# A tail in which half of each batch's base products stand behind the next batch's scan transposes, and ScalarE makes means and variances from row sums

## What is computed

```
x = x + tanh(g_xattn[0]) * L0_xattn(ctx, layernorm(x))      # scan, gated by silu(layernorm(x))
x = x + tanh(g_ffn[0])   * L0_moe(layernorm(x))             # 16 experts, top 4
x = x + tanh(g_xattn[1]) * L1_xattn(ctx, layernorm(x))
x = x + tanh(g_ffn[1])   * L1_ffn(layernorm(x))
# L1_ffn(x):  x @ base_w.T + base_b + 2 * ((x @ lora_A) * gate) @ lora_B,
#             gate = top 2 of softmax(x @ router_w.T + router_b), 8 experts of rank 16
# layernorm(x) = (x - mean) / sqrt(var + 1e-5), over the 512 channels of a token
```

## Time and profile before

| | |
|---|---|
| median of 3 runs | 1531.58 us (1530.7 to 1533.62) |
| profiled execution, its own time | 1533.84 us |
| its span, first to last instruction | 1532.0 us |
| mean granted clock of TensorE | 0.942 |

### The profile page before, as it was taken

One profiled execution on the slowest core, in us unless ns is written; L12 is line 12 of the kernel. 1 busy time (PEld: TensorE's weight loads), 2 busy tenths in 40 slices (PEclk: granted clock), 3 DMA queues, 4 the chain that ended last, 5 costly groups with the idle time before them and its releaser, 6 DMA issues.

```text
span 1532.0 us, 14502 instructions
## 1 busy us (share of the span) xinstructions
PE 1278.9 (83%) x4518; PEld 726.6 (47%) x4518; DVE 1408.5 (92%) x1468; ACT 838.0 (55%) x1344; POOL 788.3 (51%) x411
## 2 busy tenths in 40 slices
PE   7785796899699867986889999899988888836998
PEld 3331232443244323442457666566665666625555
DVE  4999999999999999998899999999899999987894
ACT  5754657574755465634865665546556444424442
POOL 0465456445644553460475456655566666555642
PEclk9898899899989998998899999999999999967999
DMA  8364456535544553460367678677786888754531
GB/s 254 107 142 126 112 131 144 136 110 140 138 139 93 143 133 100 97 171 23 90 178 235 233 244 281 228 273 234 240 262 227 276 260 289 249 191 143 169 105 56
DMA packets 99836, 264.30 MB, mean 173 GB/s; under 512 B 10832, under 2 KB 11344, under 8 KB 93616
## 3 DMA queue, kind: packets, MB, share of 16 engines
q1 hardware_dynamic: 87936, 225.36, 50.6%
q0 software_dynamic: 11440, 37.50, 7.3%
q10 hardware_dynamic: 384, 0.52, 0.1%
HBM read 233.73 MB, written 29.62 MB: 172 GB/s over the span
## 4 chain that ended last, share of the span: by engine, by line
DVE 43%; PE 22%; issue 10%; DMA 6%; POOL 5%; ACT 2%; DVEq 0%; SPq 0%; ACTq 0%; POOLq 0%
DVE state L1667 18%; DVE banks L1659 12%; PE banks L1137 7%; DMA expert_w<-in_moe_w 3%; PE banks L1148 3%; DMA ys_d<-expert_out 2%; PE banks L1047 2%; DVE y_scan L1678 2%; POOL state L451 2%; PE banks L1096 1%; PE banks L1104 1%; DVE du L1379 1%; DVE hidden L1685 1%; PE banks L1305 1%; PE banks L1116 1%
## 5 line engine op out<-in xcount | busy, mean ns | idle before, releaser
L451 POOL TENSOR_TENSOR state<-state,bc_rows 128x1024 f32<-128x1024 f32 x254 | 598.7, 2357 | 639.7 <-DVE banks L1659 639.5
L1047 PE MATMUL banks<-state,ident 128*128 128x512 f32 x640 | 332.9, 652 | 109.7 <-POOL state L451 109.6
L1667 DVE TENSOR_TENSOR_SCAN state<-decay,banks 128x1024 f32<-128x1024 f32 x176 | 402.1, 2285 | 7.5 <-ACT decay L681 3.0
L1659 DVE TENSOR_TENSOR banks<-du,bc_rows 128x1024 f32<-128x1024 f32 x256 | 314.7, 1229 | 12.8 <-issue 0.5
L1137 PE MATMUL banks<-z_gate,expert_w 128*128 128x256 f32 (+1 forms) x1504 | 284.6, 347 | 7.7 <-DMA expert_w<-in_moe_w 7.7
L1137 PEld LDWEIGHTS banks<-z_gate,expert_w 128*128 128x128 f32 x1504 | 249.7, 191 | 61.7 <-issue 20.6
L681 ACT ACTIVATE decay<-delta,neg_a 128x511 f32<-128x511 f32 x352 | 230.7, 712 | 49.2 <-DVE state L1667 45.9
L1047 PEld LDWEIGHTS banks<-state,ident 128*128 128x128 f32 x640 | 119.6, 200 | 290.4 <-POOL state L451 176.7
L1667 DVE TENSOR_TENSOR_SCAN state<-expert_w,banks 128x1024 f32<-128x1024 f32 x80 | 182.9, 2286 | 3.8 <-ACT expert_w L681 1.1
L1148 PE MATMUL banks<-expert_w,hidden 128*128 128x512 f32 x316 | 158.3, 616 | 2.9 <-DVE hidden L1688 2.9
L1678 DVE TENSOR_TENSOR y_scan<-y_scan,state 128x1024 f32<-128x1024 f32 x94 | 114.0, 1212 | 3.6 <-POOL state L451 3.6
(11 more groups left out here) (313 smaller groups left out, 1627.5 us busy)
## 6 DMA issues: line engine op xcount, KB each, us to landing
bc_rows<-bc_d SPq DMA_DIRECT2D x208, 512.0 KB
expert_w<-in_moe_w SPq DMA_DIRECT2D x48, 1536.0 KB, 9.1
ys_d<-expert_out SPq DMA_DIRECT2D x32, 512.0 KB, 10.2
ctx_t<-in_ctxT SPq DMA_DIRECT2D x8, 512.0 KB, 6.8
x_res<-in_x SPq DMA_DIRECT2D x4, 1024.0 KB, 10.6
xn_d<-y_scan SPq DMA_DIRECT2D x4, 1024.0 KB, 7.5
ys_d<-expert_out SPq DMA_DIRECT2D x15, 256.0 KB, 9.2
out_x<-x_res SPq DMA_DIRECT2D x3, 1024.0 KB, 6.1
```

The lines of the kernel that those rows point to most:

```text
L451: nc.gpsimd.tensor_tensor(W[:, c % 4], W[:, c % 4], bcast2(BC[:, u, 1, :]), ALU.mult).then_inc(mulc_done, 1)
L1047: mm = nc.tensor.matmul(PS[:, m], ID[:, :], W[:, c % 4, m, :], start=False, stop=True, skip_group_check=True)
L1659: nc.vector.tensor_tensor(drive(s), DU[:, s % 2, 2 * h:2 * h + 2, :], bcast2(BC[:, u, 0, :]), ALU.mult).then_inc(mulb_done, 1)
L1667: nc.vector.tensor_tensor_scan(flat(W[:, c % 4]), flat(DAS[c % da_slots(s, i)]), flat(drive(s)), 0.0, ALU.mult, ALU.add).then_inc(scan_don ...
```

## The change

All of it is in the tail, but for one memset of eps at VectorE's start.

1. TensorE: in rounds 1 to 3 only the base products of groups 0 and 1 stay in front of the scan transposes. Behind these come the transposes of MID, then the base products of groups 2 and 3. `stay_warm` shrinks from 14 matmuls to 4 there.
2. Statistics: VectorE's last instruction on a row (fourth combine product, or `scan_add`) also writes the row's sum (`accum_out`). ScalarE makes −mean from the sums, then squares x − mean over each row with a sum, then takes the root. VectorE only inverts it and multiplies by −mean. This replaces `tail_stats` seven times: both of batches 1 to 3 and the second of batch 0.
3. VectorE: two more combine products are taken ahead of the second norm's bias, and `lora_add` of batch b − 2 comes in the middle of batch b's combine, not at the end of round b − 1.

```diff
@@ ScalarE: in place of rstd_root @@
+            def deviations(v):
+                f = v // 2
+                if v % 2:
+                    act.wait_ge(xacc, QT * (f + 1))
+                else:
+                    act.wait_ge(combined, TOPK * QT * (f - NB + 1))
+                    act.wait_ge(yg_done, f)
+                nc.scalar.activation(NMEAN[:, v % 2, :], ROWSUM[:, v % 2, :], ACT.Copy, scale=-1.0 / D).then_inc(tail_mean, 1)
+                act.wait_ge(tail_mean, v - 2 * NB)
+                for q in range(QT):
+                    ins = nc.scalar.activation(ZS[:, q, :], X[:, f % NB * QT + q, :], ACT.Square,
+                                               bias=NMEAN[:, v % 2, q:q + 1], accum_out=SQ[:, v % 2, q:q + 1])
+                ins.then_inc(var_ready, 1)
                 act.wait_ge(var_ready, v + 1)
-                nc.scalar.activation(RS[:, :], RS[:, :], ACT.Sqrt).then_inc(std_ready, 1)
+                nc.scalar.activation(RS[:, :], SQ[:, v % 2, :], ACT.Sqrt, scale=1.0 / D, bias=EPSC[:, :]).then_inc(std_ready, 1)
@@ TensorE @@
                     base(l, 0)
                     base(l, 1)
-                    base(l, 2)
-                    base(l, 3)
-                    pe.wait_ge(midg_ready, l + 1)
-                    for q in range(QT):
-                        mm = nc.tensor.transpose(PRE[1][:, q * P:(q + 1) * P], MID[:, q, :], ID[:, :])
-                    mm.then_inc(midt_done, 1)
+                    if b == NB:
+                        base(l, 2)
+                        base(l, 3)
...
                     y_transposes(f, Y[:, b], (0, 1))
                     y_transposes(f, Y[:, b], (2, 3))
                 if l >= 0:
+                    pe.wait_ge(midg_ready, l + 1)
+                    for q in range(QT):
+                        mm = nc.tensor.transpose(PRE[1][:, q * P:(q + 1) * P], MID[:, q, :], ID[:, :])
+                    mm.then_inc(midt_done, 1)
+                    if b < NB:
+                        base(l, 2)
+                        base(l, 3)
                     pe.wait_ge(midt_ready, l + 1)
...
-                    stay_warm(PRE[1], 14)
+                    stay_warm(PRE[1], 4 if b else 14)
@@ VectorE @@
+                link(nc.vector.reciprocal(RS[:, :], RS[:, :]))
+                nc.vector.tensor_tensor(NBI[:, :], NMEAN[:, v % 2, :], RS[:, :], ALU.mult).then_inc(zn_ready, 1)
...
                 if 0 < b < NB:
-                    combine(b, QT, TOPK * QT)
+                    combine(b, QT + 2, 2 * QT + 2)
+                if b >= 2:
+                    lora_add(b - 2)
+                if 0 < b < NB:
+                    combine(b, 2 * QT + 2, TOPK * QT)
                 if l >= 0:
                     lora_logits(l)
-                if 0 < b < NB:
-                    dve.wait_ge(combined, TOPK * QT * (b + 1))
-                    dve.wait_ge(xn_ready, QT * f)
-                    tail_stats(b)
...
                     scan_add(f, range(QT), 1)
-                    dve.wait_ge(xacc, QT * (f + 1))
-                    tail_stats(b)
                     if b + 1 < NB:
-                        combine(b + 1, 2, QT)
+                        combine(b + 1, 2, QT + 2)
                     norm_bias(2 * f + 1)
-                if l >= 0:
-                    lora_add(l)
+            lora_add(NB - 1)
```

More of the change, by code:

```diff
@@ L108, in build @@
         NBI = sb("neg_mean_rstd", [P, QT])
+        ROWSUM = sb("row_sum", [P, 2, QT])
+        NMEAN = sb("neg_mean", [P, 2, QT])
+        SQ = sb("square_sum", [P, 2, QT])
+        EPSC = sb("eps", [P, 1])
         RK = sb("rank", [P, NT, NE])
@@ L203, in build @@
         hg_ready, y_done, yev, dve_step = sem("hg_ready"), sem("y_done"), sem("yev"), sem("dve_step")
+        tail_mean = sem("tail_mean")
         rows_var, rows_std, rows_zn, rows_z = sem("rows_var"), sem("rows_std"), sem("rows_zn"), sem("rows_z")
@@ L660, in rstd @@
                 rstd_exp(v)
-            def rstd_root(v):
+            def deviations(v):
[11 more added lines that the diff above has]
+                ins.then_inc(var_ready, 1)
                 act.wait_ge(var_ready, v + 1)
-                nc.scalar.activation(RS[:, :], RS[:, :], ACT.Sqrt).then_inc(std_ready, 1)
+                nc.scalar.activation(RS[:, :], SQ[:, v % 2, :], ACT.Sqrt, scale=1.0 / D, bias=EPSC[:, :]).then_inc(std_ready, 1)
             def rstd_log(v):
@@ L752, in _ @@
             act.wait_ge(a_ready, 3)
-            act.wait_ge(zeroed, 4)
+            act.wait_ge(zeroed, 5)
             conv_tap_one(0, 0)
@@ L938, in _ @@
                 elif b < NB:
-                    rstd_root(2 * f)
+                    deviations(2 * f)
                     z_gate(f)
@@ L946, in _ @@
                 if b < NB:
-                    rstd_root(2 * f + 1)
+                    deviations(2 * f + 1)
                     act.wait_ge(zn_ready, 2 * f + 2)
@@ L1460, in scan_add @@
                     xr = X[:, (f % NB) * QT + lt, :]
+                    total = ROWSUM[:, 1, lt:lt + 1] if gate else None
                     nc.vector.scalar_tensor_tensor(out=xr, in0=AUX[lt % 2], scalar=TG[:, gate:gate + 1], in1=xr, op0=ALU.mult,
-                                                   op1=ALU.add).then_inc(xacc, 1)
+                                                   op1=ALU.add, accum_out=total).then_inc(xacc, 1)
             def norm_bias(v):
                 dve.wait_ge(std_ready, v + 1)
-                nc.vector.scalar_tensor_tensor(out=NBI[:, :], in0=MV[:, :, 0], scalar=-1.0, in1=RS[:, :], op0=ALU.mult,
-                                               op1=ALU.mult).then_inc(zn_ready, 1)
+                if v < 2 * NB:
+                    nc.vector.scalar_tensor_tensor(out=NBI[:, :], in0=MV[:, :, 0], scalar=-1.0, in1=RS[:, :], op0=ALU.mult,
+                                                   op1=ALU.mult).then_inc(zn_ready, 1)
+                    return
+                link(nc.vector.reciprocal(RS[:, :], RS[:, :]))
+                nc.vector.tensor_tensor(NBI[:, :], NMEAN[:, v % 2, :], RS[:, :], ALU.mult).then_inc(zn_ready, 1)
             def rank_of(out, m, n, tri, s1, s2, nq=QT):
@@ L1708, in _ @@
                 nc.vector.memset(da, 0.0).then_inc(zeroed, 1)
+            nc.vector.memset(EPSC[:, :], EPS).then_inc(zeroed, 1)
             dve.wait_ge(masks, 6)
@@ L1867, in combine_one @@
                 xr, g = X[:, b * QT + q, :], b * QT + q
+                total = ROWSUM[:, 0, q:q + 1] if b and k == TOPK - 1 else None
                 nc.vector.scalar_tensor_tensor(out=xr, in0=gathered_row(b, q, k), scalar=CWK[:, k, g:g + 1], in1=xr,
-                                               op0=ALU.mult, op1=ALU.add).then_inc(combined, 1)
+                                               op0=ALU.mult, op1=ALU.add, accum_out=total).then_inc(combined, 1)
             sums = ((0, 0), (0, 1), (0, 2), (1, 0), (1, 1), (0, 3), (2, 0), (1, 2),
@@ L1898, in some_bias @@
                                                       op0=ALU.mult, op1=ALU.mult)
-            def tail_stats(b):
-                for q in range(QT):
-                    ins = nc.vector.bn_stats(ST[:, q, :], X[:, b * QT + q, :])
-                link(ins)
-                variances()
             v8 = lambda i: SM[:, i, 0:QT * E1].rearrange("p (q e) -> p q e", e=E1)
@@ L1985, in _ @@
                 elif b < NB:
+                    dve.wait_ge(xn_ready, QT * f)
                     norm_bias(2 * f)
```

## The result

| | before | after |
|---|---|---|
| median, range of 6 runs each on one chip | 1531.45 (1530.7 to 1533.9) | 1541.71 (1540.72 to 1544.16) |
| ratio with its 95% interval | | 1.0066 [1.0052, 1.0079] |
| profiled execution, its own time | 1533.84 | 1540.76 |
| its span | 1532.0 | 1538.7 |
| mean granted clock of TensorE | 0.942 | 0.942 |

A forecast was written before the change was run, and what follows sets the result against it. The prediction took the tail's loop between logits and gate products as the bound, with TensorE's list deciding from gate to logits. 10.5 − 2.2 + 0.5 + 2.4 + 0.6 + 3.0 = +14.8 on 1531.58 gave 1546.4 us, range 1537 to 1555.

The forecast's parts named there:

- Base products behind the scan transposes: Tail rounds 1 to 3, gate product's end to next logits products' end: TensorE's list sets 22.0, 22.0, 21.4 us, 10.5 longer.
- A to G 12.6 in each round: Tail, logits products' end to end of next batch's gate product: 12.6 us against 11.0, 14.6, 14.4, so 2.2 shorter.
- Table loads on the path at 1.28 each: ScalarE's root loads now stand behind the squares: four come onto the path, 5.1 us in the sum, without a drain.
- the rival that rested on it: A table load costs more on the path, as if ScalarE first drained: +5.1 us, 1551.5; chance 0.05.
- (a): Sum output of ScalarE's squares, 16 on the path: 0 to 3.2 us, taken as 0.15 each, +2.4.
- (b): Sum output on VectorE, on some scan adds of the path: 0 to 1.5 us, taken as +0.6.
- (c): TensorE's clock falls after its new idle 5.7 us: 0 to 1.66 us a round, taken as 1.0, +3.0.
- Batch 0, +0.5: Round 0's chain from scan add to norm grows to 5.1 us, partly offset: +0.5 us, 0 to 1.5.
- GpSimd's bias and gathers stay at nothing: GpSimd's work in the tail adds nothing, as gathers start as before and have the longer loop to land in.
- Without the cover the longer norm costs 1.5 us a round: Second norm's longer chain, rounds 1 to 3: free under late base products, otherwise about 1.5 us a round.
- VectorE's time did not fall through: Rival that VectorE's saved statistics shorten the kernel: −19.7 us, 1512; chance 0.05.
- It cancels: Rival of no change: load under the squares, free sums and clock up leave +3.7 us, 1535; chance 0.08.

The follow-up runs named there:

- e3: Changed kernel plus 24 warm-up matmuls behind the first half of TensorE's base products in rounds 1 to 3; 1537.7 us, ratio 1.0039 to the kernel before.
- e1: Kernel before with only TensorE's part of the change (moved base products and MID's transposes, warm-up 4); 1540.2 us, ratio 1.0059.
- e4: Changed kernel with group 2's base products moved back in front of the scan transposes, only four products staying behind; 1534.22 us, ratio 1.0014.
- e8: Changed kernel with 14 warm-up matmuls ahead of the row transposes in every round, as before; 1547.04 us, ratio 1.0118 to the kernel before.
- e5: Kernel before with four base products and MID's transposes behind the scan transposes in round 1 only, warm-up 4 there; 1530.54 us, ratio 1.001.
- e10: Kernel before with GpSimd's bias of batch 0 moved ahead of the gathers of batch 2; 1528.97 us, ratio 0.9998.
- e2: Changed kernel with TensorE's list of before, so statistics and VectorE's order alone; 1533.65 us, ratio 1.001 to the kernel before.
- e11: Changed kernel without GpSimd's addition of base_b, so the result lacks it; 1538.28 us, ratio 1.0051 to the kernel before.
- e12: Changed kernel with TensorE's list of before and without GpSimd's addition of base_b, so the result lacks it; 1525.95 us, ratio 0.9979 to the kernel before.
- e6: Changed kernel with three quarters of the base products in front and nine warm-up matmuls in TensorE's idle time; 1531.83 us, ratio 1.0023 to the kernel before.

## Why the prediction was right, point by point

The forecast was 1546.4 us, 14.8 above before; it is 1541.71, 10.3 above. Sign, range and mechanism hold. Two terms were nothing, and one statement that carried no number was wrong.

- **Base products behind the scan transposes: right.** The term was +10.5 with a warm clock. e3 has G to A at 21.88, 21.88 and 21.26 for the 22.0, 22.0 and 21.4 worked out, each within 0.2 us. e1 alone gives most of the loss, and each product taken out (e4) or warm-up matmul put in (e8) shows.
- **A to G 12.6 in each round: right.** 12.51, 12.86 and 12.51, the −2.2 us of the sum. The root took 0.30 us for 0.20 assumed.
- **Table loads on the path at 1.28 each: right.** Squares, load, root, load and silus follow each other within 0.03 us, so the loads did come onto the path. The further 1.38 us a switch of the Trainium skill ("ScalarE: Activation LUTs", section "What ACT_TABLE_LOAD costs") isn't seen here, and the rival that rested on it falls.
- **(a) ScalarE's sums, +2.4: mis-sized, nothing.** They have records of 0.19 us, but four squares with them take the 2.93 us of four activations. **(b) VectorE's sums, +0.6: nothing.** 0.08 us, and products start 0.67 to 0.68 us apart as without them. These two are 3.0 of the 4.5 us of the miss.
- **(c) The clock, +3.0: right in kind, too small.** 4.3 us in the loop, by e3. The Trainium skill has the effect as a pitfall: in "TensorE: Matmul & The Clock Gate", section "HAM oscillation — how this bites in real kernels", an engine that waits between bursts starts each burst cold, and rounds 1 to 3 of this tail do so: 0.50 behind 5.70, 6.05 and 5.70 us idle.
- **Batch 0, +0.5: open.** −1.0 us in the two records, but the old instructions took 21.50 us (before), 18.96 (e1), 19.41 (e5) and 19.50 (e10), the new ones 20.51 (changed), 20.54 (e2) and 20.62 (e3). Leaving out the 21.50, they cost about 1 us more, in the range given; that rests on few records.
- **"GpSimd's bias and gathers stay at nothing": wrong as a statement, right in the sum.** The bias held VectorE for over 4 us in rounds 1 and 2. It cost 0.9 us in the loop (2.3 by the ratios, which can't be told from 0.9), since the base products were later still (e11). That this cover would also hide the hold was luck: the prediction knew its 4 us of margin, not what would use it up.
- **Without the cover the longer norm costs 1.5 us a round: right only without the hold.** Against 18.09 and 16.17 us in rounds 2 and 3 e12 has 17.99 and 17.76, so −0.1 and +1.6, and in round 1 less than before. Only round 3 is a clean comparison, as the kernel before has a hold in rounds 1 and 2. With the bias in place e2 has +5.1 and +2.6. Had the change been the statistics alone, this step would have been wrong in its record's loop.
- **The rivals.** VectorE's time did not fall through: its work fell by some 19.5 us, near the 19.7 of the rival, and it stood idle for 4.14 us in front of the inverse. "It cancels" asked for three things, and one of them came, the free sums; the loads were on the path and the clock fell. The clock didn't stay down: in round 1 it was at 1.00 from 1427, in round 2 from 1464 and in round 3 from 1498, for the larger part of the moved products.

By the terms: 10.5 − 2.2 + 0 + 0 + 3.9 = 12.2 for the loop. The 3.9 is what G to A took above the worked 65.4 (69.28 − 65.4); with the clock up it takes 65.02 (e3), so it is 4.3 of clock less 0.4 by which the working was long.

## What to carry to other kernels

Ask of each wait that a change removes which engine stands behind it with a list in strict order: VectorE's 92% was worth nothing here. Three times 6.87 us of TensorE's products, less 2.24 us of warm-up each, moved from a covered stretch to one where TensorE sets the pace, 13.9 us in all, and G to A became 14.4 us longer. Where TensorE was left waiting for some 6 us it paid again, in the clock of what follows; products there that nobody reads gave 4 us back. Where an instruction of one source leaves VectorE's list and one of two SBUF sources takes its place in time, look at what GpSimd does at that moment.

## What the runs showed of the hardware

A long GpSimd `TENSOR_TENSOR` (4.5 us) holds some instructions of VectorE until it ends. Held were products with both tensors in SBUF (4.96 us in the changed kernel, 5.61 in e6 and 4.83 in e2 for 0.75; 3.00 in e10 for 0.19) and `TENSOR_SCALAR` of 128x4 (3.29 in e5, 1.04 and 0.82 in the kernel before, for 0.17). Not held were `BATCH_NORM_STATS2`, `BATCH_NORM_AGGREGATE`, `TENSOR_REDUCE` and products with a source in PSUM. The Trainium skill has this in "SBUF — State Buffer", section "Who interferes with whom": VectorE and GpSimd share a pair of ports under an exclusive lock, an instruction of VectorE with two SBUF inputs contends with a GpSimd instruction that reads SBUF, `tensor_scalar` can, and one input without such a mode does not. All rows here agree. It also says that who comes first keeps the port. In e6 VectorE's record starts 0.5 us ahead of GpSimd's and it is VectorE that waits, so the start in the profile doesn't tell who has the lock.

The accumulator reads were new too: 0.19 us on ScalarE and 0.08 on VectorE, none of it seen in the spacing of their instructions. And the clock that TensorE gets depended on more than the long idle time: in e6 a wait of 1.50 us, followed by transposes with gaps of 0.62 and 0.27 us, had 0.50 behind it too, while in e5 a wait of 1.38 us with gaps of 0.62 and 0.56 us left the logits products at the 3.87 us of a full clock.
